# A pipelined feed-forward stage: second matmuls two steps behind the first across eight batches, ranking two tiles at a time, update factors computed before a batch ends

## What is computed

```python
h = _layernorm(x) * (1 + cb) + sb                 # x: after the attention layer
scores = einsum('bsd,d->bs', h, w_router)
top_scores, top_idx = top_k(scores, 512)          # 512 of 1024 tokens, per batch
weights = sigmoid(top_scores)
sel = take_along_axis(h, top_idx)                 # 512 x 512
g = gelu(sel @ W1 + b1)                           # 512 x 2048
processed = g @ W2 + b2                           # 512 x 512
ffn = h with weights * processed added at top_idx
x = x + gb * ffn                                  # gb: one row of 512 per batch
```

## Time and profile before

| | us |
|---|---|
| median of 3 runs | 2418.35 (2418.11 to 2418.71) |
| the profiled execution, its own time | 2416.8 |
| its span, from the first to the last instruction | 2415.1 |
| PE busy | 2273.9 (94%) |
| DVE busy | 1911.6 (79%) |
| ACT busy | 1478.1 (61%) |
| POOL busy | 1371.5 (57%) |
| first feed-forward matmul | 1694.5 from the span's start |
| last feed-forward matmul ends | 2395.1 |

### The profile page before, as it was taken

The page is one execution under the profiler, slowest core; times in us unless marked ns, Lnnn a source line. Parts: engine busy times, 40 slices in busy tenths (PEclk is TensorE's granted clock), DMA queues, the critical chain, the costliest instruction groups (busy, mean ns, idle before and its releaser), DMA issues.

```text
span 2415.1 us, 41301 instructions
## 1 busy us (share of the span) xinstructions
PE 2273.9 (94%) x12772; PEld 887.0 (37%) x12772; DVE 1911.6 (79%) x2806; ACT 1478.1 (61%) x2616; POOL 1371.5 (57%) x1205
## 2 busy tenths in 40 slices
PE   6999999999999999999999999897989999999996
PEld 2333333333333333333333333231334444444442
DVE  5899899999999999999999999998744543554432
ACT  1788888888888888888888887777311111111110
POOL 4566676666756667666666666554344452543531
PEclk9999999999999999999999999999999999999998
DMA  6233333233333333323233333223612021111100
GB/s 214 68 92 77 79 82 88 72 91 72 76 87 77 84 73 90 82 70 96 67 80 97 72 79 75 67 61 97 157 44 66 22 59 52 32 57 44 57 23 18
DMA packets 123771, 180.83 MB, mean 75 GB/s; under 512 B 44112, under 2 KB 44112, under 8 KB 123480
## 3 DMA queue, kind: packets, MB, share of 16 engines
q1 hardware_dynamic: 113760, 152.30, 25.8%
q0 software_dynamic: 9728, 25.23, 3.4%
HBM read 67.17 MB, written 43.16 MB: 46 GB/s over the span
## 4 chain that ended last, share of the span: by engine, by line
PE 64%; DVE 17%; issue 8%; POOL 5%; ACT 3%; DMA 2%; SPq 1%; DVEq 0%; POOLq 0%; ACTq 0%
PE sc L558 13%; PE acc L605 13%; PE sc L747 12%; PE sc L734 12%; DVE nmax L981 10%; PE pj L568 7%; PE pj L580 5%; POOL x L1320 3%; DVE qn L1042 2%; ACT probs L810 2%; DVE stats L1024 1%; DMA room<-in_L_ffn_W 1%; PE sc L591 1%; POOL sel_rows L120 1%; DVE rinv L1037 1%
## 5 line engine op out<-in xcount | busy, mean ns | idle before, releaser
L810 ACT ACTIVATE probs<-sc,nmax 128x1024 f32<-128x1024 f32 x1024 | 1136.7, 1114 | 276.2 <-DVE nmax L981 254.8
L981 DVE TENSOR_REDUCE nmax<-sc 128x1 f32<-128x1024 f32 x1024 | 1212.6, 1215 | 61.1 <-PE sc L558 55.1
L605 PE MATMUL acc<-probs,qn 128*32 128x512 f32 x4136 | 556.7, 611 | 9.8 <-DVE x L1019 7.3
L883 ACT ACTIVATE probs<-sc,b_col 128x512 f32<-128x512 f32 x128 | 87.9, 687 | 561.6 <-PE sc L734 498.7
L568 PE MATMUL pj<-room 128*128 128x512 f16 x1536 | 395.6, 381 | 0.4 <-ACT qT L800 0.4
L747 PE MATMUL sc<-room,probs 128*128 128x512 f16 x1536 | 353.9, 380 | 8.0 <-DVE probs L1171 8.0
L558 PE MATMUL sc<-room 128*128 128x512 f16 x1024 | 310.3, 385 | 38.3 <-ACT probs L810 27.9
L558 PE MATMUL sc<-stacks 128*128 128x512 f16 x1024 | 309.5, 384 | 31.4 <-ACT probs L810 30.8
L1169 DVE CAST probs<-probs 128x512 f16<-128x512 f32 x128 | 64.6, 505 | 332.6 <-ACT probs L883 315.9
L747 PEld LDWEIGHTS sc<-room,probs 128*128 128x128 f16 x1536 | 150.0, 98 | 190.5 <-issue 7.4
L568 PEld LDWEIGHTS pj<-room 128*128 128x128 f16 x1536 | 150.2, 98 | 188.2 <-issue 9.1
(11 more groups left out here) (147 smaller groups left out, 2369.2 us busy)
## 6 DMA issues: line engine op xcount, KB each, us to landing
room<-room SPq DMA_DIRECT2D x512, 64.0 KB, 2.0
stacks<-room SPq DMA_DIRECT2D x512, 64.0 KB
h_rows<-hbuf SPq DMA_DIRECT2D x132, 128.0 KB, 2.3
out<-base SPq DMA_DIRECT2D x132, 128.0 KB, 2.5
room<-in_L_attn_x SPq DMA_DIRECT2D x96, 128.0 KB, 2.7
rows<-mod_rows SPq DMA_DIRECT2D x32, 256.0 KB, 4.1
room<-in_L_ffn_W SPq DMA_DIRECT2D x8, 1024.0 KB, 5.2
probs<-in_L_wmod SPq DMA_DIRECT2D x4, 1024.0 KB, 7.9
```

The lines of the kernel that those rows point to most:

```text
L605: mm = nc.tensor.matmul(acc[at:at + DH, :], qn[:, (p // 2) % 2, p % 2, h2, :], probs[:, (2 * p + h2) % PROBS, half * D:(half + 1) * D], st ...
L810: nc.scalar.activation(probs[:, u % PROBS, :], slot(g, ring_at(p, h2)), ACT.Exp, bias=nmax[:, u % PROBS:u % PROBS + 1], accum_out=rsum[:, ...
L883: nc.scalar.activation(g32[:, f % 2, :], ff[f % 2], ACT.Gelu_apprx_tanh, bias=b1_col[:, f:f + 1], scale=1.0 / WS).then_inc(gelu_done, 1)
L981: nc.vector.tensor_reduce(nmax[:, u % PROBS:u % PROBS + 1], slot(g, ring_at(p, h2)), AX.X, ALU.max, negate=True).then_inc(max_done, 1)
```

## The change

- **PE** runs ff2 two steps behind ff1, and across the end of a batch: the order is ff1(n, f), then ff2(n, f-2), and at f = 0 and 1 of the next batch ff2(n-1, 14) and ff2(n-1, 15). The buffer `g16` has three places for it instead of two. ff1(n, 0) waits for the low part of its tokens piece by piece (`ft_lo`), and ff2(n, 0) waits for the four PSUM tiles one by one (`acc_out`). In the last batch the last two steps are interleaved by tiles: 3 matmuls of ff2(14) and 3 of ff2(15) for each kt.
- **The transposes** for the next batch stand at f = 11 to 14, in batch 0 at f = 12 to 15.
- **DVE** ranks two tiles at each of f = 2 to 5 (in batch 0: one to two tiles at each of f = 1 to 6). `numbers` stands at f = 9, in batch 0 at 10.
- **The update** is computed as (gb * w) * result / 64 + (base + w * gb * b2). Both factors in parentheses are made by DVE at f = 15 of the batch (`update_parts`: nine instructions); when the result is there, DVE does one product (`update_scaled`) and one sum (`update_added`) per tile, at f = 1 of the next batch. POOL no longer computes in this stage; it scatters batch n-1 at the start of batch n.
- **SP** loads weight piece 6 ahead of the row stores and piece 7 behind them, and stores batch 7's scores only after `load_kept(1)`. The gb row is loaded a batch ahead.
- The places of ACT's high parts and DVE's low parts in batch 0 are moved; the first step no longer waits for ACT's warm-up instruction; the feed-forward loops are written out.

The parts of the diff that the steps below speak of (`n` is the batch; `nth(n, per, off)` is n * per + off):

```diff
@@ PE
+            def ff1(n, f):
+                if n == 0 and f == 0:
+                    pe.wait_ge(slot_free, ALL_FREED)
+                if n or f >= 2:
+                    pe.wait_ge(gelu_done, nth(n, FC, f - 1))
...
+                for t, (cc, a, z) in enumerate(terms):
+                    if f == 0 and t % 3 == 0:
+                        pe.wait_ge(ft_lo, nth(n, CC, cc + 1))
...
+                for kt in kts:
+                    if n and f == 0:
+                        pe.wait_ge(acc_out, nth(n - 1, KT, kt + 1))
...
+            for n in ORDER:
                 for f in range(FC):
-                    ff1(bb, par, f)
-                    if f >= 1:
-                        ff2_of(bb, par, f - 1)
...
+                    ff1(n, f)
+                    if f >= 2:
+                        ff2_of(n, f - 2)
+                    elif n:
+                        ff2_of(n - 1, FC - 2 + f)
+                    cc = f - KEPT_FROM[n > 0]
...
-                ff2_of(bb, par, FC - 1)
+            for kt in range(KT):
+                ff2_of(B - 1, FC - 2, [kt])
+                ff2_of(B - 1, FC - 1, [kt])
@@ ACT
+            HIGH_AT = {1: 3, 2: 4, 5: 5, 6: 6, 9: 7}
@@ DVE
+            def update_parts(n):
...
+                nc.vector.tensor_tensor(gb_b2[:], gb_row[:, par], b2_row, ALU.mult).then_inc(s_gbb2, 1)
+                for kt in range(KT):
+                    nc.vector.tensor_scalar(y[par][:, kt, :], gb_row[:, par], kept[:, par, kt, 1:2], None, ALU.mult).then_inc(y_gates, 1)
...
+                for kt in range(KT):
+                    nc.vector.scalar_tensor_tensor(out=bs[par][:, kt, :], in0=gb_b2[:], scalar=kept[:, par, kt, 1:2],
+                                                   in1=bs[par][:, kt, :], op0=ALU.mult, op1=ALU.add).then_inc(y_base, 1)
+            LOW_AT = {0: 2, 3: 3, 4: 4, 7: 5, 9: 6, 10: 7}
+            TILES_AT = {1: (0,), 2: (1, 2), 3: (3,), 4: (4,), 5: (5, 6), 6: (7,)}
@@ SP
-            for j in range(4, 6):
+            for j in range(4, 7):
                 load_weights(j)
             sp.wait_ge(post_done, NG + 1)
             store_rows(NG - 1, (NG - 1) % 2)
-            sp.wait_ge(s_dot, 2 * NG + 2)
-            store_scores(B - 1)
-            for j in range(6, 8):
-                load_weights(j)
-            sp.wait_ge(s_sc, 16 * (B + 1))
+            load_weights(7)
+
+            for n in ORDER:
+                if n + 1 < B:
+                    load_kept(n + 1)
+                if n == 0:
+                    sp.wait_ge(s_dot, 2 * NG + 2)
+                    store_scores(B - 1)
+                    sp.wait_ge(s_sc, 16 * (B + 1))
```

More of the change, by code:

```diff
@@ L365, in block_phases, with nth @@
         KEPT_AT = (6, 9, 12, 14)
[L367 to L379 removed]
+        ORDER = range(B)
+        KEPT_FROM = (FC - CC, FC - CC - 1)
+        def nth(n, per, off):
+            return n * per + off
         def only(per, off):
@@ L1217, in ffn @@
-                    if f > FC - CC:
-                        cc = f - (FC - CC) - 1
-                        kept_low(nb, npar, cc, aux[cc % 2])
-                if not last:
-                    kept_low(nb, npar, CC - 1, aux[(CC - 1) % 2])
-                if first:
-                    for i in range(2):
-                        dve.wait_ge(s_st[i], 128 * (NG // 2 + i) + 16)
-                dve.wait_ge(ff2_pe, n_of(bb, par, FC, FC))
-                dve.wait_ge(s_b, 32)
-                for kt in range(KT):
-                    nc.vector.scalar_tensor_tensor(out=y[par][:, kt, :], in0=ff2[kt], scalar=1.0 / WS, in1=b2_row,
-                                                   op0=ALU.mult, op1=ALU.add).then_inc(acc_out, 1)
@@ L1230, in ffn @@
-                if not last:
-                    return
-                for kt in range(KT):
-                    if kt == 0:
-                        dve.wait_ge(s_gbs[par], bb * (16 * KT) + 16 * KT)
-                    dve.wait_ge(y_gb, n_of(bb, par, KT, kt + 1))
-                    nc.vector.scalar_tensor_tensor(out=y[par][:, kt, :], in0=y[par][:, kt, :], scalar=kept[:, par, kt, 1:2],
-                                                   in1=bs[par][:, kt, :], op0=ALU.mult, op1=ALU.add).then_inc(y_done, 1)
@@ L1241, in _ @@
+                    if n + 1 < B and 0 <= cc < CC:
+                        kept_low(n + 1, cc, aux[cc % 2])
+                    if f == FC - 1:
+                        update_parts(n)
+            for kt in range(KT):
+                update_scaled(B - 1, kt)
+                update_added(B - 1, kt)
         @block.gpsimd
@@ L1429, in _, with scatter @@
             gather_base(0, out_rows[0:T])
-            def ffn(bb, par, first, last, peeled):
-                if not last:
-                    wait_alone(r.s_slot, n_of(bb, par, 1, 2))
+            def scatter(n):
+                for kt in range(KT):
+                    wait_alone(y_done, nth(n, KT, kt + 1))
+                    nc.gpsimd.indirect_dma_start(out_rows, bass.IndirectOffsetOnAxis(kept_i[:, n % 2, kt:kt + 1], 0),
+                                                 y[n % 2][:, kt, :], None).then_inc(s_out[n % 2], 16)
```

299 lines of the change are left out of this document (129 added, 170 removed).

## The result

The changed kernel takes 2397.13 us (median of four runs, 2393.09 to 2398.88), the kernel before 2418.23 in the same comparison (2417.39 to 2418.71): a ratio of 0.9917, 95% interval 0.9902 to 0.9932. That is 21.1 us less, where 28.6 were forecast; the time lies in the stated range of 2385.5 to 2400, but outside the 2386 to 2394 of the forecast itself, and close to the price of Rival A (2399.4). The profiled run took 2397.25 us, with a span of 2395.5.

A forecast was written before the change was run, and what follows sets the result against it. PE's own work was taken to bound batches 1 to 7, but not batch 0 or the tail. Savings of 1.05 + 6.7 + 14.4 + 6.5 = 28.6 us from 2418.35 gave 2389.8 us; own range 2386 to 2394, stated 2385.5 to 2400.

The forecast's parts named there:

- Rival A: Batch 0: small writes of batch 7's score store hold batch 1's gather, landing 8 us later; 2399.4 us, chance 0.17.
- The start: First matmul ff1(0) waits for the last exp and not ACT's warm-up; minus 1.05 us.
- The ends of batches: Between batches PE no longer waits for the split or finds anything late; the whole 6.7 us go.
- The tail: After PE's last matmul: 13.5 us instead of 20.0, minus 6.5 us.
- the lower bound of 3.5: Tail: saving only 3.5 us if scatters beside DVE's two-tensor instructions took 2 us more.
- Batch 0: First batch: PE loses 4.0 us instead of 18.4 by waiting for batch 1's gathered rows; minus 14.4 us.
- The rows: +8.6: Batch 0: gathered rows of batch 1 land 8.6 us behind the numbers, at 1759.3 us.
- leave the clock as it is: Batch 0: no clock loss counted, since the gaps were said to be under 2.80 us.
- the gap of 3.6 us: Batch 0: PE's wait at the transposes for batch 1's gathered rows, 1759.3 - 1755.7, bounds 2.7 and 5.7.
- the 1.5 us at ff2(4): Batch 0: earlier PE loss to a late split, ready at 1723.5 and not 1722.0, counted within the 3.6 us.
- Rival B: Batch 0: weight piece 5 or 6 lands late, delaying gelu and the slots by some 6 us; 2397.8 us, chance 0.12.
- Rivals C and D: C: batch-end or tail gain absent, 2396.4 us, 0.06. D: PE meets `acc_out` at every boundary, about 2456 us, 0.03.

The follow-up runs named there:

- parts_late: Against the changed kernel: update factors of batches 0 to 6 computed in the next batch's step 1, right before use; 2425.73 us.
- store_later: Against the changed kernel: batch 7's scores stored only after the gathered rows of batch 1 have landed; 2386.47 us.
- rows_last: Against the changed kernel: stores of batch 0's updated rows issued behind weight piece 7, not ahead of it; 2395.28 us (one run).
- store_twice: Against the changed kernel: batch 7's scores stored twice in a row at the same place; 2397.28 us (one run).
- store_wide: Against store_later: the same 4 KB also written ahead of the gather, as 128 pieces of 32 bytes, to an unread row; 2387.92 us.

## Why the prediction was right, and which term was not

- **The whole**: 28.6 us forecast, 21.1 found. The time is in the range because the range took in Rivals A and B up to 2400; the forecast itself, 2386 to 2394 at a chance of 0.60, did not come, and Rival A did. Three of the four terms came as worked out, and the largest one came at little more than a quarter.
- **The start**: 1.05 forecast, 1.1 found behind the last attention group.
- **The ends of batches**: all 6.7 us went, and PE finds everything there as the timeline of the mechanism had it (no wait for a split, some 2.5 us of room at `acc_out`). `parts_late` shows that room: 4.8 us put in its way gave gaps of 2.4. Of the lag one step would do. Whether the crossing was needed, or the end of POOL's products alone would have sufficed, stays open.
- **The tail**: 6.5 forecast, 7.2 found. The scatters are not held by DVE's sums (1.02 and 0.97 us), so the lower bound of 3.5 did not come. The 0.7 are two errors that partly cancel: the last scatter starts 1.15 us behind DVE's last sum (0.3 forecast), and from its start to the end of the span it is 7.2 us and not 9.0.
- **Batch 0**: a gain of 14.4 us forecast, 4.0 found. This step failed: of the 18.4 us lost before, the batch was to lose 4.0 and still lost 14.4. From the start of ff1(0) the slots came at 40.1 us (42.0 forecast), the numbers at 59.1 (57.2), the rows at 73.7 (65.8). The term "The rows: +8.6" was the main fault: it took 14.6, because the 8.6 of the kernel before was measured with no small store ahead of the gather; with the store moved away in `store_later` it is 8.9 (1753.65 to 1762.56). That is 6.0 us of the difference, and the later numbers are 1.9. The half clock behind the wait at the transposes is another 3, which "leave the clock as it is" had set to nothing. Its reason did not hold in its own terms: the gap of 3.6 us that the same paragraph gives is above the 2.80 it is compared with, unless the 1.5 us at ff2(4) come first, and that late split cost only 0.2. Less the 0.4 of tenths that the forecast had in it, these make the 10.4. `store_later` took away 8.4.
- **Rival A** named this mechanism, its place and its price (+10, less 0.4), with a chance of 0.17, and its sign came: a gather that lands over 10 us behind its numbers. Found are +9.0 in the profile (span 2395.5 against 2386.5) and +7.3 on the median; the profiled execution lay 1.6 us under the median of the kernel before and 0.1 above that of the changed one. The row that spoke for it, the piece that took 16.2 us behind the same store in the earlier trace rows, deserved more weight than the row stores that I held against it. `rows_last` shows, in one run, that these slow a piece by some 2.4 us.
- **Rival B**: piece 6 took 11.2 us to land and ACT stood 7.9 for it; PE lost 2.7 + 1.6 us there, but the slots were not late (its sign was slots behind 1740), and with the gather as the last to come none of it showed in the time.
- **Rivals C and D** did not come. D's threshold is near, though: `parts_late` crosses it with one line moved, at about 4 us an end.

What stays open: why small pieces hold the transfers of other queues that are moved behind them. The runs show that it is so with 1024 scattered pieces of 4 bytes and not with 128 of 32, and that the pieces themselves had gone out some 12 us before the store completed, but not the mechanism.

## What to carry to other kernels

When a stage is moved earlier, follow every queue that it is moved past: here the ranking came 8 us sooner, and a store that used to lie far ahead of a gather was moved right in front of it by the same change and cost as much again. A duration read from a trace, such as "8.6 us from numbers to rows", holds only with the same neighbours in the queues; ask which new neighbour the change gives it. When two waits follow one another toward the same late transfer, removing the first gives nothing; find what lands last, and move its consumer or its obstacle.

## What the hardware showed that was not expected

- A store of 1024 pieces of 4 bytes to memory takes 11.3 (`rows_last`) to 13.6 us (1749.20 to 1762.77 in the changed kernel) to complete ahead of the gathers and 9.0 behind them (`store_later`), the same 4 KB in 128 pieces of 32 bytes 1.7 us. In the changed kernel its pieces are recorded within 2 us of its issue. Gathers that move behind the first kind crawl until it is done, at 28 to 37 GB/s in the changed kernel and 9 to 45 in `store_twice`, where they move at 211 without it.
- Gaps of 2.5 and 2.7 us left TensorE at 2.4 GHz in `store_later`, one of 3.5 in `store_wide` too; one of 2.72 in the changed kernel did not, and gaps of 2.37 us in `parts_late` brought it to 1.2 GHz for a while at six ends of batches (11.3 us lost in all) and not at the first. The length of a gap alone does not say whether the clock falls.
